# Earlier key and value weights, four pairs folded before the first scores, and zeros by rows: one change to a two-layer attention and expert kernel

## The reference, cut to what matters

```python
x = x + memory_concat(ctx, layernorm(x))        # shift rows, a convolution (rate 4) makes 16 compressed rows a batch
x = x + ffn0(layernorm(x))                      # shared expert + top 2 of 8 experts, hidden 128, sqrt(softplus) weights
x = x + xattn(layernorm(x), ctx_1024, ctx_1024) # 16 heads of 64, 64 context rows a batch
x = x + ffn1(layernorm(x))                      # top 2 of 8 experts, hidden 384, SiLU gate
```

## Time and profile before

| | us |
|---|---|
| median of 3 runs | 814.96 (814.42 to 817.94) |
| the profiled execution, its own time | 822.08 |
| its span | 820.2 |
| TensorE busy | 749.1 (91%) |
| VectorE busy | 530.4 (65%) |
| ScalarE busy | 489.3 (60%) |
| GpSimd busy | 429.7 (52%) |
| granted TensorE clock, mean | 0.98 |

### The profile page before, as it was taken

How to read it: one execution, slowest core, us unless ns; L and a number is a source line. 1 busy time by engine, 2 the same in 40 slices (tenths; PEclk the granted TensorE clock), 3 DMA queues, 4 the chain that set the end, 5 groups by cost and what they waited for, 6 DMA issues and landing times.

```text
span 820.2 us, 16199 instructions
## 1 busy us (share of the span) xinstructions
PE 749.1 (91%) x4633; PEld 653.7 (80%) x4633; DVE 530.4 (65%) x1423; ACT 489.3 (60%) x1379; POOL 429.7 (52%) x399
## 2 busy tenths in 40 slices
PE   4799987889898499999999999789999999999996
PEld 3546635676776399999998988689999999999995
DVE  5687857552665488888889888776543343365454
ACT  2337735555676488888877787356555454454541
POOL 3000655564687958888545778544652445333220
PEclk9899999999999799999999999899999999999998
DMA  8999997787899943663610444633444434565457
GB/s 248 343 285 308 332 300 257 241 276 227 184 268 241 320 121 81 163 153 70 210 63 2 161 163 148 206 104 120 140 137 142 144 104 133 179 210 177 161 178 233
DMA packets 128745, 154.47 MB, mean 188 GB/s; under 512 B 10875, under 2 KB 118550, under 8 KB 127638
## 3 DMA queue, kind: packets, MB, share of 16 engines
q1 hardware_dynamic: 102896, 112.55, 44.7%
q0 software_dynamic: 18624, 34.29, 15.8%
q10 hardware_dynamic: 7142, 6.59, 2.4%
HBM read 77.39 MB, written 76.00 MB: 187 GB/s over the span
## 4 chain that ended last, share of the span: by engine, by line
PE 70%; DVE 8%; issue 5%; ACT 5%; POOL 5%; DMA 4%; DVEq 1%; another core or an unknown queue 0%; SPq 0%; POOLq 0%; ACTq 0%
PE psum L849 24%; PE psum L1164 9%; PE psum L1142 8%; PE psum L1236 7%; PE psum L1241 6%; PE psum L1237 6%; POOL X L718 4%; PE psum L1152 3%; PE psum L1252 3%; ACT pr L1549 2%; PE psum L1215 2%; DMA X<-yl_dram,slots_y 1%; DMA yk_dram<-ys,L 1%; PE psum L1037 1%; PE psum L942 1%
## 5 line engine op out<-in xcount | busy, mean ns | idle before, releaser
L771 POOL DMA_INDIRECT yk_dram<-ys,L x52 | 53.6, 1031 | 136.2 <-ACT ys L1641 136.0
L718 POOL DMA_INDIRECT X<-yl_dram,slots_y x64 | 101.0, 1578 | 31.9 <-issue 14.2
L690 POOL DMA_INDIRECT xs_dram<-N,slots x64 | 65.9, 1029 | 97.0 <-DVEq L1943 58.4
L1549 ACT ACTIVATE pr<-psum,nmx 128x64 f32<-128x64 f32 x512 | 108.4, 365 | 6.8 <-DVE nmx L2314 6.6
L1236 PE MATMUL psum<-whi,xTh 128*128 x284 | 103.9, 366 | 3.4 <-ACT xTh L1603 2.4
L2410 DVE TENSOR_TENSOR hs<-psum,hs 128x384 f32<-128x384 f32 x71 | 39.7, 559 | 87.4 <-PE psum L1241 45.2
L1237 PE MATMUL psum<-wlo,xTh 128*128 x284 | 96.0, 338 | 0.0
L759 POOL DMA_INDIRECT xs_dram<-N,slots x64 | 69.7, 1090 | 35.9 <-ACT ys L1641 19.1
L1241 PE MATMUL psum<-whi,xTl 128*128 x284 | 74.1, 342 | 1.5 <-DVE xTl L2433 1.4
L751 POOL TENSOR_TENSOR pr<-pr,sm 128x1024 f32<-128x1024 f32 x32 | 62.2, 1944 | 19.5 <-DVE sm L2321 17.3
L1633 ACT ACTIVATE hs<-psum 128x384 f32<-128x384 f32 x71 | 34.9, 492 | 49.0 <-PE psum L1241 36.7
(11 more groups left out here) (370 smaller groups left out, 2041.2 us busy)
## 6 DMA issues: line engine op xcount, KB each, us to landing
fx<-xs_dram SPq DMA_DIRECT2D x78, 130.0 KB
yl_dram<-fy SPq DMA_DIRECT2D x78, 128.0 KB
xs_dram<-fill SPq DMA_DIRECT2D x4, 2340.0 KB, 14.1
xs<-xs_dram SPq DMA_DIRECT2D x71, 130.0 KB
wlo<-in_L_ffn_W_dram SPq DMA_DIRECT2D x4, 1536.0 KB, 11.4
xs_dram<-cz SPq DMA_DIRECT2D x1, 5070.0 KB, 24.2
xs_dram<-cz SPq DMA_DIRECT2D x7, 650.0 KB
X<-in_x_dram SPq DMA_DIRECT2D x4, 1024.0 KB, 11.7
```

The source lines that it names most:

```text
L690: po.indirect_dma_start(XS, bass.IndirectOffsetOnAxis(ap=slot[k][:, t:t + 1], axis=0), N0[:, t, :], None).then_inc(s[done], 16)
L718: po.indirect_dma_start(X[:, t, :], None, YL[b // 2], bass.IndirectOffsetOnAxis(ap=slot_y[k][:, t:t + 1], axis=0), compute_op=ALU.add).the ...
L771: po.indirect_dma_start(YK, bass.IndirectOffsetOnAxis(ap=yid[:, j:j + 1], axis=0), ys[j % YB], None).then_inc(s[f"y_out{j % YB}"], 16)
L1549: last = act(pr[b][:, S * h:S * h + S], bank[2 * b + h // 8][:, S * (h % 8):S * (h % 8) + S], ACT.Exp, bias=nmx[:, h:h + 1])
```

## The change: what it does

**Loads.** SP asks for Wk and Wv right behind the memory rows of batch 0, ahead of those of batch 1 and of the convolution's weights. Wo has a semaphore of its own (`wo_in`), which the first value fold waits for; `keys_values` waits for Wk and Wv alone (`kv_in`). SP sends pair 0 ahead of the x rows of batches 2 and 3; the other pairs stay behind the zeros of group 0.

**Order.** The Q products come ahead of the transposes of `U`. `fold` is split into `fold_keys` and `fold_values`; the convolution (`memory`) stands behind the key fold of pair 0, the memory rows behind `keys_values(1)`. Four pairs (`FIRST_FOLDS`) are folded ahead of `scores(0)`, and pair 4 stands between it and `ranks(0)` / `softplus(0)`.

**Zeros.** The eight zero transfers of group 1 go. VectorE computes after `choose(1)`, in `padding()`, which slots no row of group 1 fills (7 times 128 of them); POOL writes zeros there with seven indirect transfers behind the group's last rows, and SP waits for them (`padded`) before it loads group 1's slots.

```diff
 sp.dma_start(wq_sb, wq...).then_inc(s["wq_in"], 16)
 memory_rows(0)
+for dst, src in ((wk_sb, wk), (wv_sb, wv)):
+    sp.dma_start(dst, src...).then_inc(s["kv_in"], 16)
 memory_rows(1)
 for c in range(DC):
     sp.dma_start(convw_sb[:, :, c, :], ...).then_inc(s["cw_in"], 16)
-for dst, src in ((wk_sb, wk), (wv_sb, wv)):
-    sp.dma_start(dst, src...).then_inc(s["kvo_in"], 16)
 x_rows(0)
-sp.dma_start(wo_sb, wo...).then_inc(s["kvo_in"], 16)
+sp.dma_start(wo_sb, wo...).then_inc(s["wo_in"], 16)
 x_rows(1)
...
-sp.wait_ge(s["kvo_in"], 16 * 3)
+sp.wait_ge(s["wo_in"], 16)
 for b in (2, 3):
     memory_rows(b)
-sp.wait_ge(s["pre_c_tp"], 4)
+folded(0)
 for b in (2, 3):
     x_rows(b)
...
-for j in range(PAIRS):
...
-    sp.dma_start(rows_of[1][:, parts[j]:parts[j + 1], :],
-                 zeros.to_broadcast([P, parts[j + 1] - parts[j], XW])).then_inc(s["zeroed1"], 16)
+for j in range(1, PAIRS):
+    folded(j)
...
                 if g:
+                    sp.wait_ge(s["padded"], 16 * PADS)
                     sp.dma_start(vraw, VD[0]...).then_inc(s["v_in"], 16)
...
+                if g:
+                    po.wait_ge(s["pads"], 1)
+                    for i in range(PADS):
+                        po.indirect_dma_start(
+                            XS, bass.IndirectOffsetOnAxis(ap=pad_at[:, i:i + 1], axis=0),
+                            zero4, None).then_inc(s["padded"], 16)
...
             keys_values(0)
-            fold(0)
-            fold(1, False)
+            fold_keys(0)
+            memory()
+            keys_values(1)
+            memory_rows()
+            fold_values(0)
+            for j in range(1, FIRST_FOLDS):
+                fold(j)
             scores(0)
-            keys_values(2)
-            keys_values(3)
+            fold(FIRST_FOLDS)
             ranks(0)
-            fold(2, False)
-            for j in range(3, PAIRS):
+            for j in range(FIRST_FOLDS + 1, PAIRS):
                 fold(j)
...
+            def padding():
+
+                base, e_ = LS * P, E * LT
+                counts, cum, open_, at = (ta[:, 2 * E * k:2 * E * k + E] for k in range(4))
+                at = at[:, 0:PADS]
+                c3 = wk12[:, 0:PADS * E].rearrange("p (i e) -> p i e", e=E)
+                last_t = tc_[:, e_:2 * e_].rearrange("p (e t) -> p e t", e=E)[:, :, LT - 1:LT]
+                nc.vector.tensor_copy(counts.rearrange("p (e a) -> p e a", a=1), last_t)
+                nc.vector.tensor_tensor_scan(cum, ones8[:, :], counts, 0.0, ALU.mult, ALU.add)
+                tt(cum, counts, cum, ALU.subtract)
+                stt(open_, te[:, :], float(P), cum, ALU.mult, ALU.add)
+                tt(c3, bc(pad_no, E), rep(open_, PADS), ALU.is_ge)
+                tt(c3, c3, rep(counts, PADS), ALU.mult)
+                nc.vector.tensor_reduce(at, c3, AX.X, ALU.add)
+                stt(pad_at, at, float(base), pad_no, ALU.add, ALU.add)
+                ve.sem_inc(s["pads"], 1)
```

More of the change, by code:

```diff
@@ L87 @@
 DEEP = 3
+PADS = LS - 2 * LT
+FIRST_FOLDS = 4
 XB, YB = 8, 4
@@ L1350, in _, with memory, memory_rows @@
                 last.then_inc(s["wqt_sb"], 1)
-            ac.wait_ge(s["pre_c_tp"], 4)
-            act(C, bank[4][0:S, 0:D], ACT.Copy).then_inc(s["pre_c_sb"], 1)
-            ac.wait_ge(s["pre_c_tp"], 5)
-            for h in range(2):
-                last = act(araw[96:P, 2 + h, :], bank[5 + h][96:P, :], ACT.Copy)
-            last.then_inc(s["pre_c_sb"], 1)
-            ac.wait_ge(s["consts"], 3)
+            ac.wait_ge(s["pre_c_tp"], 3)
+            act(UT, bank[4].rearrange("p (c n) -> p c n", c=DC), ACT.Copy).then_inc(s["pre_c_sb"], 1)
+            ac.wait_ge(s["consts"], 3)
+            table(0, ACT.Ln)
+            def memory():
+                ac.wait_ge(s["pre_c_tp"], 4)
+                act(C, bank[4][0:S, 0:D], ACT.Copy).then_inc(s["pre_c_sb"], 1)
+            def memory_rows():
+                ac.wait_ge(s["pre_c_tp"], 5)
+                for h in range(2):
+                    last = act(araw[96:P, 2 + h, :], bank[5 + h][96:P, :], ACT.Copy)
+                last.then_inc(s["pre_c_sb"], 1)
             def keys_values(j):
@@ L1379, in fold, with fold_out @@
                     keys_values(j + 1)
-                for i in range(4):
+                fold_out(j, range(4))
+            def fold_out(j, sides):
+                for i in sides:
                     ac.wait_ge(s["a_p" if i < DC else "vw_p"], DC * j + i % DC + 1)
                     if j >= DEEP:
-                        ac.wait_ge(s[f"st_out{i}{j % DEEP}"], 16 * (j // DEEP))
+                        ac.wait_ge(s[f"st_out{i // 2}{j % DEEP}"], 16 * 2 * (j // DEEP))
                     bk_, sc = (bank[2 + i], DH ** -0.5) if i < DC else (bank[3 + i], 1.0)
@@ L1424, in shared_out @@
                 elif q == 2:
-                    ac.wait_ge(s["st_out00"], 16 * len(range(0, PAIRS, DEEP)))
+                    ac.wait_ge(s["st_out00"], 16 * 2 * len(range(0, PAIRS, DEEP)))
                 for h, k in enumerate((6, (5, 4)[q // LQ])):
@@ L1480, in _ @@
             keys_values(0)
-            fold(0)
-            fold(1, False)
+            fold_out(0, (0, 1))
+            memory()
+            keys_values(1)
+            memory_rows()
+            fold_out(0, (2, 3))
+            for j in range(1, FIRST_FOLDS):
+                fold(j)
             scores(0)
-            keys_values(2)
-            keys_values(3)
+            fold(FIRST_FOLDS)
             softplus(0)
-            fold(2, False)
-            for j in range(3, PAIRS):
+            for j in range(FIRST_FOLDS + 1, PAIRS):
                 fold(j)
```

98 lines of the change are left out of this document (56 added, 42 removed).

## The result

The change takes 832.85 us (median of 4 runs, 831.43 to 833.07) against 816.39 for the kernel before (4 runs, 814.42 to 817.94): the ratio is 1.0218, with a 95% interval of 1.0181 to 1.0255, or some 16.5 us. The profiled execution of the change took 832.78 us, with a span of 831.0. Against the profiled execution of before (822.08) that is only 10.7 more: the profiled execution after lies at its median, the one before lay 5.7 above its own.

What follows compares the result with a forecast made beforehand. It took TensorE's start and VectorE's unbroken 40.42 us up to group 1's scores as the bound; 7.4 + 0.9 - 0.7 + 1.4 + 1.4 = +10.4 on 822.08 gave 832.5, less 7.1 is 825.4 us, range 816.5 to 830.5.

Steps and rivals of the forecast that it cites:

- part 1: Loads and order before the first scores: first transposes move from 50.20 to 57.6, +7.4 us (4.3 to 9.4).
- the value fold of pair 0 takes 4.9: TensorE before the first scores: pair 0's value fold runs from 36.1 to 41.0, taking 4.9 us as in the profile before.
- the difference is carried over: Last step of the sum: the profiled execution's 7.1 us above the median is kept, turning 832.5 into 825.4.
- Part 2: Copies out and softplus of group 0: softplus ends at 84.8 where VectorE needs it at 83.9, +0.9 us (0 to 3).
- Part 3: Group 1's scores: two groups of products at the low clock, +2.0, against an unexplained 2.7 us wait gone: -0.7 us.
- Part 4: List of empty rows: eight VectorE instructions ahead of the slot stage, 2.5 us, partly covered by a 1.09 us wait: +1.4.
- under 52: Sign that the prediction is wrong: the slot stage, 139 to 196 before, takes less than 52 us.
- The rival that hung the waits on the zero writes: Scores and slot stage: zero writes stalled other engines, so their waits vanish and the change is not slower, 810.4; chance 0.10.
- Part 5: Zeros by rows: seven POOL scatters end at 200.4, ahead of group 0's collecting, +1.4 us (0 to 3); slot loads covered.
- The early start holds most of it back: Rival on the start: TensorE reaches its floor, +3.6, the list is hidden and scatters end in time, 818.6; chance 0.15.
- pair 4's copies come late: Rival on softplus of group 0: late landing of pair 1 delays it and VectorE, 3 instead of 0.9, 827.5; chance 0.07.
- Scatters at their slowest: Rival on POOL's zeros: all seven take 2.2 + 0.3 us instead of 1.26, +8.7, 834.1; chance 0.06.

Runs made afterwards that it cites:

- busy-gap experiment: The changed kernel with six throw-away TensorE products in its 1.25 us gap ahead of the first value fold: 845.18 us, ratio 1.0163 to the kernel before.
- no-pauses kernel: The kernel before without pauses between group 1's 32 scatters: ratio 1.0009 on a chip of the first kind (about 815 us), 1.0330 on the second (827 to 831).
- order-alone kernel: The changed kernel with two folded pairs ahead of the first scores instead of four, and group 1's block zeroed in full by SP, no zero scatters: ratio 1.0052, +3.8 us.
- the zeros alone: The kernel before with only group 1's zero block replaced by the list of empty rows and seven scatters, issued last: 1.0143, 1.0071 and 1.0121 on second-kind chips.

## Why the prediction was wrong

The sign was right. 832.85 lies above the range (to 830.5) and 7.5 above the forecast.

**The step that failed in the kernel itself is in part 1: "the value fold of pair 0 takes 4.9".** It took 8.1, since the prediction gave the wait of 1.1 us ahead of it no effect on the clock. With the slow turn of pair 1 behind it this is 4.9 of the 12.7 us at the start, the largest term that was missed. **The other step that failed is the last one of the sum, "the difference is carried over":** the profiled execution of the change was forecast at 832.5 and took 832.78, but its median is 832.85 too, not 7.1 lower. The 7.1 us (5.7 against the later median) belonged to one execution of before and to its waits, not to a profile as such. Parts 3 and 5 lean on the same waits.

That 832.5 was so near is luck: two terms were too small by 5.3 and 3.0, and the slot stage, for which nothing was forecast, gave 4.1 back. Against typical executions of before the change costs 16.5 and not 10.4:

- *Part 1, first scores +7.4 (4.3 to 9.4).* Measured +12.7, above the upper bound. The value fold starts at 36.52 (36.1 forecast), and pairs 2 and 3 go by at 5.17. The term that was mis-sized is "the value fold of pair 0 takes 4.9": it took 8.1, and pair 1's turn behind it 6.9 in place of 5.2, at 1.2 GHz. The 0.4 us later start, 3.2 and 1.7 are the 5.3 that were missing. The prediction had priced the lower clock only for the gap before 27.0, where it did not fall, and gave the 1.1 us wait for ScalarE no clock at all. The busy-gap experiment shows the cause and its price, 4.8 us.
- *Part 2, copies and softplus +0.9.* Measured 0: the stretch is 40.34 us.
- *Part 3, group 1's scores -0.7.* Measured -0.7 (12.6 to 11.9): 1.4 us more for cold transposes, and a wait gone. In the no-pauses kernel, which is before up to there, the same stretch takes 14.9 us (103.16 to 118.08), against 17.4 in the first trace of before and 16.7 in the change, so this -0.7 is no gain of the change.
- *Part 4, the list +1.4.* Its eight instructions take 2.0 us, and the first slot goes from 11.9 to 12.8 later: +0.9.
- *The slot stage*, for which nothing was forecast: 53.0 us before, 48.9 after, the "under 52" that the prediction named as a sign against it. The rival that hung the waits on the zero writes looks borne out by this, yet two kernels that write all zeros, on a chip of the first kind, contradict it: the order-alone kernel has 49.1 us there and the no-pauses kernel 47.3. The change's 48.9 is what is usual on that kind, and before's 3.29 and 2.90 were that execution's.
- *Part 5, the scatters +1.4 (0 to 3).* Durations right (0.96 + 0.30, one of 1.55), and the collecting starts right behind them, as forecast. But it is 13.1 later where the last slot was 8.7 later: +4.4. The step took the 7.78 us that POOL waited in before as cover, and 2.4 of them were the wait ahead of the last slot (189.39), without which that slot comes 1.5 us behind the one before it, as in the change and in the order-alone kernel, and not 3.9. In the order-alone kernel POOL waits 5.47 us there, and its last send starts 0.3 us after the last slot is turned (190.00 and 189.74), as in the change 0.6 after (201.50 and 200.91); in before it started 1.9 ahead of it (190.34 and 192.22). The rest of the 3.0 is one slow scatter, 0.6. The slot loads, "covered", come 17 us later; group 1's first slot is then 12.8 later, so no more than the rest, and that much was right. POOL in the order-alone kernel:

```profile
190.00 0.96 POOL L699 DMA_INDIRECT xs_dram<-N,slots  x1 [0.31 <-issue]
196.43 2.44 POOL L727 DMA_INDIRECT X<-yl_dram,slots_y  x1 [5.47 <-DMA yl_dram<-fy]
```

**The rivals.** *The early start holds most of it back* and *pair 4's copies come late*: no, the first transposes came 12.7 us later and VectorE's stretch did not grow. *Scatters at their slowest* (2.2 us each): no; their issue is the same on the chips of both kinds. The Trainium skill, SBUF — State Buffer, "SBUF: two separate sides", has VectorE's copies hold GpSimd's descriptors up. What the runs show on the second kind of chip is the reverse: POOL keeps its 0.96 us and the other three engines are late. Neither the forecast nor a rival had a case in which scatters slow the slots, worth 6 to 12 us there for seven. On the first kind, where the result was measured, the zeros alone were never run; that they cost about the 4.4 us of the table is read from traces and not shown by an experiment. From the last slot to the collecting it is 6.9 us in before, 6.7 in the order-alone kernel and 11.3 in the change.

Without what was only that execution's: 12.7 at the start, 1.4 for the cold transposes, 0.9 for the list and 4.4 for the scatters are 19.4; the collecting and attention give 0.6 and 1.7 back (the last rows of the table), and 17.1 stands against the 16.5 between the medians. This is a sum of readings from single executions, so it is as near as that by good fortune too.

## What to carry to other kernels

Before a profile's execution is used as a base, compare it with the median of the runs: waits without a named releaser may be its own, and neither a gain, nor a discount, nor cover for other work may be hung on them. Price a wait of TensorE ahead of a long run of products with the clock behind it: 1.25 us of standing cost 4.8 us here, and work for nothing in the gap brought them back, but only as long as no other wait follows. And where a part of a change is to hide in an engine's idle time, read that idle time in more than one execution and ask what made it long.

## What the runs showed of the hardware

- After the gap of 1.25 us the granted clock fell to 1.2 GHz 1.2 us into the next work and stayed there for 10.2 us (37.7 to 47.9), though TensorE was busy throughout. After before's gap of 4 us it came back 3.9 us after the work had begun (the earlier trace rows is its low part). The Trainium skill, TensorE: Matmul & The Clock Gate, "HAM oscillation — how this bites in real kernels", describes a kernel whose clock falls back again with every wait for a transfer; the rows here agree that a wait brings the clock down, and the wait was of 1.25 us.
- The same program takes 815 us on some chips and 827 to 831 on others, and the difference is not even: 32 indirect transfers in one run cost nothing that can be told from noise on one kind (+0.7, interval -1.1 to +2.5) and 28 us on the other. The kernel's pauses between them, two scatters at a time, are worth nothing on the first and 28 us on the second, one chip of each having been measured. Why is open. In the second pair of stretches above the DMA engines are busy 0.47 and 0.30 of the time, so they are not full. By the records the products of a slot end at 164.9 there and ScalarE's copy of them starts at 173.94, after an idle time of 8.70 us without a named releaser. Neighbouring rows or every seventh row made no difference.
